# Attention output turned by a DMA and projected in half precision, and another split of the softmax work between ScalarE and VectorE

## The reference

```python
q, k, v = (split_heads(x @ W + b) for W, b in ((Wq, bq), (Wk, bk), (Wv, bv)))   # x is layer-normed
scores = jnp.einsum('bhqd,bhkd->bhqk', q, k) / np.float32(np.sqrt(HD))
scores = jnp.where(adj[:, None, :, :] > 0, scores, jnp.float32(NEG))
attn = jax.nn.softmax(scores, axis=-1)
out = jnp.einsum('bhqk,bhkd->bhqd', attn, v)
out = out.transpose(0, 2, 1, 3).reshape(b, n, D_OUT)
return out @ Wo + bo
```

## Time and profile before

| | us |
|---|---|
| median of 3 runs | 1326.36 (1326.15 to 1327.17) |
| profiled execution | 1322.85 |
| its span, first to last instruction | 1321.0 |
| attention stage in it | about 40 to 603 |
| granted TensorE clock over the span | 0.947 of full speed |

### The profile page before, as it was taken

How to read it: one execution, slowest core, us unless ns; L and a number is a source line. 1 busy time by engine, 2 the same in 40 slices (tenths; PEclk the granted TensorE clock), 3 DMA queues, 4 the chain that set the end, 5 groups by cost and what they waited for, 6 DMA issues and landing times. The chain is left out here.

```text
span 1321.0 us, 39795 instructions
## 1 busy us (share of the span) xinstructions
PE 1093.3 (83%) x12580; PEld 785.2 (59%) x12581; DVE 995.3 (75%) x2407; ACT 866.2 (66%) x1705; POOL 853.4 (65%) x897
## 2 busy tenths in 40 slices
PE   0789999999999999994389999799999999989100
PEld 0456666666666666663167677577777777768100
DVE  3468888888888888885486888587777777767398
ACT  0577788888888888882277788567666666568000
POOL 3125677777778777776676677277777777766300
PEclk9999999999999999998699999999999999999755
DMA  2112333333333333222345554344444444334399
GB/s 76 29 47 71 86 90 91 94 92 94 94 96 93 81 88 93 74 60 69 95 121 143 140 158 116 65 94 100 101 101 93 98 96 96 79 67 80 114 355 306
DMA packets 276549, 136.54 MB, mean 103 GB/s; under 512 B 195142, under 2 KB 254700, under 8 KB 276474
## 3 DMA queue, kind: packets, MB, share of 16 engines
q1 hardware_dynamic: 242938, 93.39, 29.3%
q0 software_dynamic: 16896, 33.86, 8.2%
q10 hardware_dynamic: 16640, 8.39, 2.1%
HBM read 47.95 MB, written 54.04 MB: 77 GB/s over the span
## 5 line engine op out<-in xcount | busy, mean ns | idle before, releaser
L1377 POOL DMA_INDIRECT pairs_dram<-x_rows x272 | 279.1, 1026 | 123.4 <-issue 80.8
L1055 ACT ACTIVATE hid<-Z,biases 128x512 f32<-128x512 f32 (+1 forms) x336 | 207.9, 631 | 139.9 <-PE Z L1023 86.2
L1070 DVE SCALAR_TENSOR_TENSOR h<-hid,h 128x512 f16<-128x512 f32 (+1 forms) x288 | 183.5, 650 | 53.6 <-ACT h L1046 49.2
L474 DVE TENSOR_REDUCE smin<-S 128x8 f32<-128x1024 f32 x128 | 155.8, 1217 | 88.9 <-PE S L740 87.4
L1035 PE MATMUL Y<-w,h 128*128 (+1 forms) x3168 | 193.6, 221 | 11.6 <-DVE h L1070 8.7
L1035 PEld LDWEIGHTS Y<-w,h 128*128 128x128 f16 x3168 | 186.2, 99 | 28.4 <-issue 11.9
L1168 POOL DMA_INDIRECT slots_dram<-x_rows,pair_slot x128 | 132.4, 1034 | 48.2 <-issue 23.0
L1023 PE MATMUL Z<-x_rows,w 128*128 128x512 f16 (+1 forms) x720 | 147.5, 351 | 11.5 <-DMA x_rows<-slots_dram 5.9
L335 POOL DMA_INDIRECT slots_dram<-x_rows,pair_slot x116 | 118.7, 1023 | 29.1 <-issue 16.6
L477 DVE TENSOR_TENSOR probs<-smin,S 128x768 f32<-128x768 f32 x128 | 122.1, 954 | 14.4
L1046 ACT ACTIVATE h<-hid 128x512 f16<-128x512 f32 (+1 forms) x176 | 105.8, 601 | 21.0 <-ACT hid L1055 5.6
(11 more groups left out here) (212 smaller groups left out, 2192.0 us busy)
## 6 DMA issues: line engine op xcount, KB each, us to landing
y_pairs<-pairs_dram SPq DMA_DIRECT2D x32, 512.0 KB, 6.1
x_res<-in_x_dram SPq DMA_DIRECT2D x32, 256.0 KB, 3.3
adj<-in_adj_dram SPq DMA_DIRECT2D x32, 256.0 KB
xT_dram<-xT SPq DMA_DIRECT2D x32, 256.0 KB, 3.4
xTu<-xT_dram SPq DMA_DIRECT2D x32, 256.0 KB
out_dram<-x_res ACTq DMA_DIRECT2D x16, 512.0 KB, 10.7
pairs_dram<-x_rows POOLq DMA_INDIRECT x272
slots_dram<-x_rows,pair_slot POOLq DMA_INDIRECT x256, 2.5
```

The source lines that it names most:

```text
L474: dve.tensor_reduce(smin[:].rearrange("p (r e) -> p r e", e=2), S_heads, AX_X, ALU.min).then_inc(s["min_done"], 1)
L1055: act.activation(self.hid[:, c, 0:w], self.bank(b, c)[:, 0:w], ACT.Gelu, bias=bias[:, c:c + 1], scale=1.0 / (XS * WS)).then_inc(self.gelu_ ...
L1070: dve.scalar_tensor_tensor(out=self.piece(b)[:, 1, c, 0:w], in0=self.hid[:, c, 0:w], scalar=HS, in1=self.piece(b)[:, 0, c, 0:w], op0=ALU.m ...
L1377: pool.indirect_dma_start(pairs_dram, bass.IndirectOffsetOnAxis(ap=pair_of[n][:, j:j + 1], axis=0), y_sb[n % NY][:, j], None, bounds_check ...
```

## The change

The output's way is another one. ScalarE copies the four tiles of `attn` to fp16 (`high_output`), VectorE subtracts to get the low half (`low_output`), SyncE turns both halves of all four tiles with one DMA (`turn_output`) into `aT16`, and out is three fp16 matmuls per tile with `wo16`. V is no longer divided by 64, so that `attn` carries that factor; the residual addition divides it out. Only the last group is still transposed by TensorE. `attn` has one buffer instead of two. The normed x of a group is turned by one DMA instead of four.

`SHIFTED` is 4: VectorE subtracts for four heads, and ScalarE takes four heads' exponentials straight from the scores.

The jobs of M0 are placed otherwise: lg (now of the group four steps back) before the first transposes of tile 0, out at the end of tile 0, Q, K and V at the ends of tiles 1, 2 and 3. On ScalarE V is emptied at the start of the next tile 0, `high_output` ends tile 2, `high_half` moves ahead of the second `pT` copy of tile 3. On VectorE the second norm's statistics move from tile 3 to tile 2, the mask from tile 2 to tile 3. GpSimd sends all but the first scatter after `norm1`.

```diff
-SHIFTED = 6
+SHIFTED = 4
...
+        def turn_output(g):
+            wait(sp, "asplit_done", g + 1)
+            wait(sp, "out_ps", g)
+            sp.dma_start_transpose(aT16[:, :, :, :].rearrange("p j a t -> p (j a) t"),
+                                   at16[:, :, :, :].rearrange("p j a c -> p (j a c)")).then_inc(s["aT_in"], 16)
...
             store_xT(g - 6)
+            if g - 4 < NG - 1:
+                turn_output(g - 4)
             if g - 1 < NG:
                 turn_normed(g - 1)
...
+        def low_output(g):
+            wait(dve, "ahi_done", g + 1)
+            dve.tensor_tensor(at16[:, :, 1], attn[:, :, :, :].rearrange("p j h c -> p j (h c)"), at16[:, :, 0],
+                              ALU.subtract).then_inc(s["asplit_done"], 1)
...
+                if j == 3 and has(g, 1):
+                    low_output(g - 1)
...
-                if j == 2 and has(g, -1):
-                    mask(g + 1, 1 - q)
-                if j == 3 and has(g, 2):
+                if j == 2 and has(g, 2):
                     stats2(g - 2)
                     gather2(g - 2)
+                if j == 3 and has(g, -1):
+                    mask(g + 1, 1 - q)
...
+        def high_output(g):
+            wait(act, "norm_done", (g + 1) * GT // 2)
+            wait(act, "aT_in", g * 16)
+            act.activation(at16[:, :, 0], attn[:, :, :, :].rearrange("p j h c -> p j (h c)"), ACT.Copy)\
+                .then_inc(s["ahi_done"], 1)
...
+                if j == 2 and has(g, 1):
+                    high_output(g - 1)
...
+                    wait(pe, "aT_in", (g + 1) * 16)
...
                 for j in range(GT):
-                    mm = pe.matmul(bank[:, j * P:(j + 1) * P], attnT[:, j * P:(j + 1) * P], wo[:], start=False, stop=j == GT - 1)
+                    for n, (k, m) in halves():
...
-                tasks = {0: (None, ("aT", g - 2, q), None), 1: (None, ("out", g - 2, q), None),
-                         2: (("Q", g + 1, 1 - q), ("K", g + 1, 1 - q), None),
-                         3: (None, ("V", g + 1, 1 - q), ("lg", g - 3, 1 - q))}[j]
+                tasks = {0: (("lg", g - 4, q), None, ("out", g - 2, q)), 1: (None, None, ("Q", g + 1, 1 - q)),
+                         2: (None, None, ("K", g + 1, 1 - q)), 3: (None, None, ("V", g + 1, 1 - q))}[j]
```

More of the change, by code:

```diff
@@ L84, in attention_phase @@
     xn16 = sb("xn16", [P, GT, 2, P], F16)
-    xnT = sb("xnT", [P, 2, 2, GT * P], F16)
+    xnT = sb("xnT", [P, 2, GT, 2, P], F16)
     QT = sb("QT", [P, 2, GT * P])
@@ L91, in attention_phase @@
     oT = sb("oT", [P, 2, P])
[L92 to L96, removed]
+    attn = sb("attn", [P, GT, H, HD])
+    at16 = sb("at16", [P, GT, 2, P], F16)
+    aT16 = sb("aT16", [P, GT, 2, P], F16)
+    wo16 = sb("wo16", [P, 2, P], F16)
+    wq, wk, wv, bias_rest = (attn[:, n].rearrange("p h c -> p (h c)") for n in range(GT))
+    bo_rows, bv_mat, out_bias, ones = (at16[:, n].rearrange("p a c -> p (a c)").bitcast(F32) for n in range(GT))
+    before = aT16[:, 0].rearrange("p a c -> p (a c)").bitcast(F32)
     xc2 = xn
@@ L463, in normalise @@
             if j == 0:
-                wait(dve, "aT_ps", g - 1)
-            dve.tensor_tensor(attn[:, q, j:j + 2].rearrange("p j h c -> p (j h) c"),
+                wait(dve, "asplit_done", g)
+            dve.tensor_tensor(attn[:, j:j + 2].rearrange("p j h c -> p (j h) c"),
                               ON_heads[:, :, :, 0:HD].rearrange("p j h c -> p (j h) c"),
@@ L551, in drain @@
             choose(a - 2, 0)
+            wait(dve, "ahi_done", NG)
+            dve.tensor_tensor(aT16[:, :, 1], last_aT, aT16[:, :, 0], ALU.subtract).then_inc(s["asplit_done"], 1)
             residual(b, LAST[b, "out"])
@@ L621, in step @@
                     evac(*a)
+                if j == 3 and has(g, -2) and not (isinstance(g, int) and g < 0):
+                    high_half(g + 2)
                 if has(t, 1, NT):
@@ L630, in step @@
                     act.activation(oT[:], OD[:, 0:2 * P].rearrange("p (a t) -> p a t", a=2), ACT.Copy).then_inc(s["o_sb"], 1)
-                if j == 3 and has(g, -2) and not (isinstance(g, int) and g < 0):
-                    high_half(g + 2)
+                if j == 2 and has(g, 1):
+                    high_output(g - 1)
         def drain():
@@ L663, in m0_task @@
                 if task == "Q":
-                    wait(pe, "xnT_in", (g + 1) * GT * 16)
+                    wait(pe, "xnT_in", (g + 1) * 16)
                 m0_free(pe, task, step_g)
@@ L667, in m0_task @@
                 for n, (k, m) in halves():
-                    mm = pe.matmul(M0[:, :], w16[:, k], xnT[:, q, m], start=n == 0, stop=n == 2)
+                    mm = pe.matmul(M0[:, :], w16[:, k], xnT[:, q, :, m], start=n == 0, stop=n == 2)
                 mm.then_inc(s["q_ps" if task == "Q" else "k_ps"], 1)
@@ L673, in m0_task @@
                     for n, (k, m) in halves():
-                        mm = pe.matmul(M0[:, j * P:(j + 1) * P], xnT[:, q, m, j * P:(j + 1) * P], wv16[:, k],
+                        mm = pe.matmul(M0[:, j * P:(j + 1) * P], xnT[:, q, j, m], wv16[:, k],
                                        start=n == 0, stop=n == 2)
@@ L692, in m0_task @@
                     m0_free(pe, task, step_g)
+                else:
+                    wait(pe, "sub_done", NT)
+                    wait(pe, "direct_done", NT)
+                if isinstance(g, int) and g == NG - 1:
+                    wait(pe, "asplit_done", NG)
+                else:
+                    wait(pe, "aT_in", (g + 1) * 16)
                 pe.matmul(bank[:, :].rearrange("p (j c) -> p j c", j=GT), sel[:],
@@ L695, in m0_task @@
                 for j in range(GT):
-                    mm = pe.matmul(bank[:, j * P:(j + 1) * P], attnT[:, j * P:(j + 1) * P], wo[:], start=False, stop=j == GT - 1)
+                    for n, (k, m) in halves():
+                        mm = pe.matmul(bank[:, j * P:(j + 1) * P], aT16[:, j, m], wo16[:, k],
+                                       start=False, stop=j == GT - 1 and n == 2)
                 mm.then_inc(s["out_ps"], 1)
```

67 lines of the change are left out of this document (31 added, 36 removed).

## The result

| | before | after |
|---|---|---|
| median, us | 1326.55 (1326.15 to 1327.17) | 1439.57 (1433.13 to 1452.99) |
| ratio | | 1.0865 [1.0785, 1.0945] |
| profiled execution, us | 1322.85 | 1452.99 |
| its span, us | 1321.0 | 1451.1 |
| end of the attention stage in it (SyncE's first load of the next stage), us | 632.27 | 753.27 |

The account below looks back on a forecast made before the run. TensorE was taken as bound by a fixed chain per tile with filled holes. Uncovered jobs (1.86 us a step) and the aT wait (1.45) made 95 us with the stage's ends, giving 1421 us, range 1370 to 1485.

Parts of the forecast that it names:

- The bound: Attention stage, TensorE: a fixed chain per tile with filled holes; PT1 to PT2 stays 1.3 to 1.4 us.
- Rival 3: TensorE bound by its work, not the chain: removed work saves 0.75 us a step, 1303 us; chance 0.08.
- The jobs at the tiles' ends: TensorE: jobs moved from gaps to uncovered tile ends; tiles 5.25, 4.65, 4.3, 4.95 us, step 19.15 without DMA wait.
- Tile 3: Last tile of a step: 3.65 us base, rank 0.3, V 0.68, late pT copy 0.35; together 4.95 us.
- The wait for aT: TensorE's output job waits about 1.45 us per step for the transposed aT, giving a period of 20.6 us.
- rival 2: SyncE: the merged transposition issues in 5.0 us, four times a small one; step 22.5, 1484 us; chance 0.12.
- The landing: The transposition's data, queued behind three transfers, land 10.75 us after tile 3's scores; bounds 10.3 to 10.9.
- the two ends: Attention stage outside the 22 steps from tenth to last mask load: 22 of the 95 us forecast.
- The merged transposition "gains nothing": SyncE: one DMA for the normed x frees 3.75 us a step, but xnT lands in time anyway; no gain.
- The split of the exponentials "no gain, no loss": Four heads subtracted on VectorE, four direct on ScalarE: limit for next scores moves from 3.6 to 3.7 us.

Follow-up runs that it names:

- e1: Changed kernel with the output's transposition issued first in SyncE's loop, ahead of mask load, x load and store of xT: 1384.83 us.
- e2: Changed kernel with the M0 jobs put back in the gaps between the transposes, SyncE's queue unchanged: 1325.18 us.
- e4: Changed kernel with the edits of both e1 and e2, jobs in the gaps and output's transposition first: 1320.22 us.
- e7: e1 with the place operations ahead of the low half in VectorE's tile 3: 1379.15 us.
- e11: Kernel before with only the merged transposition of the normed x, one DMA instead of four: 1313.44 us.
- e3: Kernel before with SHIFTED = 4 alone: 1333.32 us.
- e10: e6 with SHIFTED = 4, all else the same: 1313.04 us.
- e6: e5 with place operations before the low half, high_output moved to tile 3, high_half, mask and statistics moved back: 1305.39 us.
- e5: e4 with SHIFTED = 6: 1363.67 us.
- e12: Changed kernel with SHIFTED = 6 alone: 1467.16 us.

## Why the prediction was right, point by point

1421 us, 1370 to 1485, slower with 0.90: 1439.57 us came, slower, 18.6 us above the forecast. The two causes that it names, uncovered jobs and a late aT, are the two that e1, e2 and e4 show. Their size was short: the step is 22.0 us and not 20.6, so 4.7 us longer than before and not 3.3.

- **The bound.** Right. A chain PT1, copy, PT2 with filled holes: 1.40 us between them with no job in the gap, 1.62 with all of out in it (e2). Rival 3, work as the bound, needed PT2 0.7 us behind PT1; it is refuted, and e2 shows the cover directly.
- **The jobs at the tiles' ends.** Right as a mechanism, 0.17 and 0.58 us short in two tiles and 0.26 long in one. Against the forecast, in e1 where nothing else disturbs: tile 0 4.99 (5.25), tile 1 4.82 (4.65), tile 2 4.29 (4.3), tile 3 5.53 (4.95); together 19.63 (19.15). Through the stage that is 22 steps of 2.34 us, 51.5, between the tenth and the last mask load; up to the tenth e1 loses 4.8 us and behind the last 5.6. Its stage ends 61.9 us later than that of before.
- **Tile 3, the term that was mis-sized.** The forecast had VectorE's low half end at 3.9 us after the scores with the place operations behind it, and drew from that only when the mask is ready. But TensorE's V product needs the first of these operations. Timeline of after:

```profile
415.78 0.71 PE L770 MATMUL S<-KT,QT 32*128 32x256 f32 x8
...
418.16 0.65 ACT L639 ACTIVATE pT<-PT 128x512 f32<-128x512 f32 x1
...
418.86 0.66 PE L800 MATMUL PT<-ident,probs 128*128 128x128 f32 x4 [1.01 <-ACT pT L639]
419.03 0.68 DVE L452 TENSOR_TENSOR at<-attn,at 128x512 f16<-128x512 f32 x1
419.63 0.18 DVE L526 TENSOR_TENSOR eq<-OD,pick 128x32 f32<-128x32 f32 x1
...
419.96 0.65 PE L812 MATMUL OD<-pT,V 128*32 128x128 f32 x16 [0.44 <-DVE eq L526]
...
420.13 0.41 DVE L474 TENSOR_SCALAR negmask<-adj 128x512 bf16<-128x512 f32 x1
...
421.31 0.71 PE L770 MATMUL S<-KT,QT 32*128 32x256 f32 x8
```

  The first copy starts at 2.38 (2.45 forecast), the low half ends at 3.93 (3.9), the mask at 4.76 (4.8), but the V product starts 0.44 late and the tile is 5.53 long. L526 reads OD, which the next V product writes; this dependency was not followed to TensorE. e7 confirms it: with the place operations first, tile 3 is 0.40 us shorter. That the step gains only 0.08 there is because the next tile 0 then waits for V's copy.
- **The wait for aT.** Right in mechanism and place. The transposition starts 6.37 us after the scores of tile 3 (6.4 forecast) and issues in 1.3 to 1.5 us, so rival 2, with 5.0, is refuted. It lands 11.4 after them and not 10.75. In these two steps TensorE waits 1.8 us, over the stage between 1.3 and 1.9 with a mean of 1.64, where 1.45 was forecast. The landing was the estimate with the widest bounds: 4.35 was taken from issue to landing, a median of 4.7 was measured.
- **The clock, not foreseen.** A step at full clock is 21.1 to 21.5 us. The longest is made of tiles of 6.82, 4.82, 4.30 and 5.53. Against the forecast's 20.6 that is 0.12 + 0.17 + 0 + 0.58. The mean step is 22.0; the rest is in steps like the second of the windows above, with TensorE at 1.2 GHz behind the wait. The forecast has no term for it. Of the 121 us of the profiled execution, 14.7 are lost up to the tenth mask load, 100.7 in the 22 steps from there to the last, and 5.6 behind it. The forecast had 95 in all, 22 x 3.3 = 72.6 for these steps and 22 for the two ends: the ends were right, the steady steps are 28 us short. That execution is the slowest of the four, 13 us above their median, and 9 us of it can be the later stages. That the runs of after spread over 20 us, with mean clocks of 0.928 to 0.938, fits a clock that falls in some steps and not in others, but only one execution has its trace.
- **The merged transposition "gains nothing".** Wrong in the kernel before, by 8 us (e11). It holds for mid-stage, as the unchanged period shows, and the start of the stage was not read for it. What it does in after is open.
- **The split of the exponentials "no gain, no loss".** Nearly: four heads cost 7.8 us in e3 against before and 7.7 in e10 against e6.

## What to carry to other kernels

When a chain of short dependent steps bounds an engine, the holes in it are where the engine's other work is free. Moving work from a hole to the chain's end costs its whole duration, and makes a result wanted earlier. Before a transfer is put behind others in a queue, count to the landing and not only to the issue, and read the first steps of a stage apart from its steady ones.

Where one engine's operation is longer than all its rows elsewhere, look which operation of another engine ends with it or runs beside it: such a collision can lock in a loop (L516 and L520 in e5, the mask in e12), and shifting one unrelated instruction can free it.

## What the runs showed of the hardware

- **The clock falls behind a short wait that returns each step.** In after TensorE waits 1.3 to 1.9 us for aT once in 22 us (once 2.2) and is busy 355.6 of the 460 us from 100 to 560; the granted clock of this stretch is 0.96, and 0.50 in the 6 us behind one such wait, where the eight score matmuls of a tile take 1.24 us instead of 0.71. It falls in about every second step, behind waits (1.3 to 1.9 us) that are not longer than those without a fall. In e1, e2 and e4, where that wait is absent or short, the stretch has 1.00; it also has it in e5, where TensorE waits some 1.2 us a step for a subtraction. So a wait of 1.3 to 1.9 us may cost 1 to 2 us more.
- **VectorE's operations can take several times as long beside GpSimd's.** 0.19 us becomes 0.73 or 1.07 us (e5), 0.70 for L516 in e1. These two read two tensors of SBUF; L526, with one of its two inputs in PSUM, stays at 0.18 in after, e1 and e5. The mask of e12, which goes from 0.42 to 0.87 us, reads only one tensor, so two inputs are not the only case. The Trainium skill, page "SBUF — State Buffer", section "Who interferes with whom", says that a VectorE instruction with two SBUF inputs contends with a GpSimd instruction that reads SBUF; the rows of L516 and L520 agree.
- **A wide transposition issues as fast as a narrow one:** 128x1024 in half precision from SBUF takes 1.23 us with no transfer issued ahead of it (e1, median of 23), against 1.25 for 128x256. Behind other transfers it takes longer: 1.54 for aT and 1.94 for xnT in after (medians, 100 to 560 us). It lands 3.1 us after the start of its issue with nothing ahead; for the last small one of the earlier trace rows, 1.25 and 1.15 give about 2.4.
